# A two-layer mixture of experts on one core: the last group's down products two slots sooner, routing in single slots, first weights from ScalarE's queue, FFN tiles shared anew

## The chip, the cores and the metric

The kernel runs on one core of a Trainium2 chip. The time is the device time of one execution in microseconds (us). The engines are TensorE (PE in the profile, PEld for its weight loads), VectorE (DVE), ScalarE (ACT), GpSimd (POOL) and SyncE (SP, which here only issues transfers).

## The reference

There are 32 samples of 128 tokens with 128 channels, all in fp32. Two layers each add an FFN output to x:

```python
x = x + _L0_ffn_ref(_L0_cond_ref(x, cond_1024, ...), ...)
x = x + _L1_ffn_ref(_L1_cond_ref(x, cond_1024, ...), ...)
```

- Layer 0's first half gives each sample two of four experts by a gate: `out += w_be * mask[e] * (gelu(x @ ew1[e] + eb1[e]) @ ew2[e] + eb2[e])`, and adds a shared expert `gelu(x @ sw1 + sb1) @ sw2 + sb2`.
- Layer 0's second half runs eight experts on every token, `silu(x @ w_gate) * (x @ w_up) @ w_down`, weighted per token by the product of two softmaxes, normalized.
- Layer 1's first half has two shared silu experts and eight routed gelu experts, of which each token takes two by a sigmoid router.
- Layer 1's second half is a low-rank FFN: `gelu((x @ U1) @ V1 + b1) @ U2 @ V2 + b2`.

## The kernel before

The tokens stand as 8 blocks of 512 columns. Every matmul operand is split into a high and a low part (fp32r), and each product takes three matmuls: high by high, weight low by input high, weight high by input low. The work is a list of tiles, `plan()`, of 128 hidden channels by 512 columns. A tile goes up (its product lands in one of four PSUM banks, `zb`), through an activation, is split into `HH` and `HL` (two of the three other engines), and goes down (three matmuls, two in layer 1) into an output bank.

The kinds of tiles, in program order: A (the shared expert of layer 0, blocks 0 to 5), G (19 groups of four samples, gathered by expert, 4 tiles each), A again (blocks 6 and 7), B (8 experts by 8 blocks by 4 tiles), then S, R and F (layer 1: shared, routed, and the final low-rank FFN with tiles f = 0 to 3 per block).

Order is set by slots. Slot k holds, on TensorE, first the small products that stand in tables for k (`route_a` and others), then the up product of tile k, then the down product of tile k - LAG, with LAG = 5. The other engines walk the same slots in their own programs, each strictly in its own order. k0 below is the slot in which the last group's (G18's) first tile goes up; the A tiles of block 6 go up at k0+4 to k0+7, those of block 7 at k0+8 to k0+11, and B's first at k0+12.

What hangs on the last group: after its fourth down product at slot t_g (before: k0+8), VectorE forms `TMP` (L1266: bank plus bias, times the mask and weight `WM`), GpSimd adds it to four samples in `AC` (L1479, four adds), and only then may the routing matmuls of layer 0 read `AC` (L755, in `route_a`, from slot t_g+3 on) and ScalarE and VectorE split `AC` into the `XH` and `XL` of B (L911 and L1291, `split_a`). `WM` for the group is made by GpSimd (L1463) in the slot five after the group's second tile went up; this place is not changed. The routing of four blocks feeds a softmax (`soft_a`, `exp_a`, L919).

An `inplace` tile is activated within its PSUM bank, and its bank is free only when its `HL` is written. Any other tile's activation goes to `Hf`, which has NS = 4 places by tile number modulo 4, so that tile n waits for the `HL` of tile n - 4. `hi_act` says that ScalarE writes `HH` (L968), else VectorE does (L1395); `lo_pool` says that GpSimd writes `HL` (L1469), else VectorE does (L1398). In the F tiles of the last three blocks (`LATE` = 5), tiles 0 and 2 have `HH` from VectorE and `HL` from GpSimd; tile 1 is in place with `HH` from ScalarE and `HL` from VectorE; tile 3 is in place with both from VectorE. These twelve tiles are the end of the program.

At the start, SP issues x's first block, the first half of the first weights, the small constants and the second half of those weights, then the rest of x. TensorE runs two fp32 matmuls on zeros (`WARM`, L706), for which GpSimd clears part of `AC` (L1404). The first product needs x split by VectorE (L1278, L1280) and the weights split by ScalarE (L897) and VectorE (L1283).

Of the kernel before, what the change touches and what calls it, by code (L numbers as in the profile page):

```python
# [12 lines left out]
NB = 32  # L13
NT = NB * P
BLK = 512
NBLK = NT // BLK
SEG = (0, 42, 86, 128)
LATE = NBLK - 3
LAG = 5
# [17 lines left out]
AW = 1024  # L37
# [6 lines left out]
NGRP = 19  # L44
NPAIR = 4 * NGRP
FRONT = 6
# [8 lines left out]
class Item:  # L55


    def __init__(self, kind, blk, ex, f, last):
        self.kind, self.blk, self.ex, self.f, self.last = kind, blk, ex, f, last
        self.cols = BLK  # L60
        self.inplace = kind in "AG" or (kind == "F" and blk >= LATE and f % 2 == 1)

# [50 lines left out]
def build(nc, x_d, small_d, pack_d, wa_d, wb_d, wc_d, wf_d, scr_d, wup_d, wdown_d, out_d):  # L113
    with ExitStack() as ctx:
# [39 lines left out]
        AC = sb("AC", [P, NB + 4, P], F32, actx)  # L154
# [34 lines left out]
        f_wa = [sem(f"f_wa{i}") for i in range(5)]  # L189
# [7 lines left out]
        s_zero = sem("s_zero")  # L197
# [23 lines left out]
        items = plan()  # L221
# [4 lines left out]
        real = [it for it in items if it]  # L226
        for n, it in enumerate(real):
            it.n = n
        pos = {(it.kind, it.blk, it.ex, it.f): it for it in real}

        def done(kind, blk, ex, f):
            return pos[kind, blk, ex, f].k + LAG

        t_g = done("G", NGRP - 1, 0, 3)
# [5 lines left out]
        def when(times, after=0):  # L240
            return {t + after: b for b, t in enumerate(times)}

        split_a = {t_g + 3 + b: b for b in range(NBLK)}
        route_a = {t_g + 3: (0,), t_g + 4: (1,), t_g + 5: (2, 3), t_g + 8: (4,), t_g + 9: (5,), t_g + 10: (6,),
                   t_g + 12: (7,)}
        logit_a = {t + 1: v[-1] // 4 for t, v in route_a.items() if v[-1] % 4 == 3}
        lag_b = [t + (4 if b % 4 == 3 else 5) for b, t in enumerate(t_b)]
        split_b, route_b, logit_b = when(t_b, 2), when(lag_b), when(lag_b, 1)

        soft_a = {t_g + 6: 0, t_g + 14: 1}  # L250
        soft_at = {}
# [40 lines left out]
        read = {}  # L292
        for it in real:
            if it.last and it.kind in "AGB":
                late = 3 if (it.kind, it.blk, it.ex) == ("B", 0, 0) else 0
                read.setdefault(it.k + LAG + late, []).append(it)


        z_users = []
        for k in range(slots):  # L300
            if k < len(items) and items[k]:
                it = items[k]
# [7 lines left out]
        for it in real:  # L310
            if it.kind in "BS":
                n_prod[it.n] = len(n_prod) + 1
            if it.kind == "R":
                n_gated[it.n] = len(n_gated) + 1
            it.hi_act = it.kind in "BS" or (it.kind in "AG" and it.k % (8 if it.k < 16 else 4) != 0) or (
                it.kind == "F" and (it.f == 1 if it.blk >= LATE else it.k % 2 == 1)) or (it.kind == "R" and it.ex % 4 != 3)
            it.lo_pool = (it.kind == "B" and it.k % 4 == 1) or (
# [200 lines left out]
        stage_a = [ST[:, 0, 0:AW], ST[:, 1, 0:AW], CWB[:, 0, 0:AW], CWB[:, 0, AW:2 * AW], CWB[:, 1, 0:AW]]  # L518
# [48 lines left out]
        def sync_program(e):  # L567
            e.dma_start(XT[:, 0, :], x_d[:, 0:BLK]).then_inc(f_x[0], 16)
            e.dma_start(stage_a[0][:, 0:512], wa_d[:, 0:512]).then_inc(f_wa[0], 16)
            e.dma_start(sm[:, 0:SOON], small_d[:, 0:SOON]).then_inc(f_sm, 16)  # L570
            e.dma_start(stage_a[0][:, 512:AW], wa_d[:, 512:AW]).then_inc(f_wa[1], 16)
            for b in range(1, NBLK):
# [8 lines left out]
            for k in range(slots):  # L581
# [53 lines left out]
                if k in fill_b:  # L635
                    ex = fill_b[k]
# [28 lines left out]
                if k in add_y:  # L665
                    b = add_y[k]
                    e.wait_ge(*ab_done.of(("y", b)))
                    e.dma_start(out_d[:, b * BLK:b * BLK + BLK], CB[:, b % 2, :]).then_inc(f_out[b], 16)
                if LAG <= k < len(items) + LAG and items[k - LAG]:
                    it = items[k - LAG]  # L670
# [32 lines left out]
        def tensor_program(e):  # L703
# [4 lines left out]
            for k in range(slots):  # L708
# [53 lines left out]
                if k in route_b:  # L762
                    b = route_b[k]
# [24 lines left out]
                if k in last_mm:  # L788
                    b = last_mm[k]
# [4 lines left out]
                if k < len(items) and items[k]:  # L794
                    up(e, items[k])
                if LAG <= k < len(items) + LAG and items[k - LAG]:
                    down(e, items[k - LAG])

# [91 lines left out]

        def scalar_program(e):
            e.wait_ge(s_zero, 1)
            e.activation(q1[0:NB, :], AC[0:NB, 4 * FRONT, :], ACT.Gelu_apprx_tanh)
# [9 lines left out]
            for k in range(slots):  # L903
# [3 lines left out]
                if k in split_a:  # L907
                    b = split_a[k]
# [12 lines left out]
                if k in split_b:  # L921
                    b = split_b[k]
# [7 lines left out]
                if k in low_rank:  # L930
                    b = low_rank[k]
# [471 lines left out]
        def gpsimd_program(e):  # L1403
            e.memset(AC[:, 4 * FRONT:NB + 4, :], 0.0).then_inc(s_zero, 1)  # L1404
            e.wait_ge(s_wa_hi, 2)
# [174 lines left out]
```

## Time and profile before

| | us |
|---|---|
| median of 3 runs | 905.75 |
| lowest and highest | 904.97 and 907.12 |
| the profiled execution's own time | 907.58 |
| its span (first to last instruction) | 905.5 |
| TensorE busy | 882.8 |
| VectorE busy | 688.2 |
| ScalarE busy | 574.8 |
| GpSimd busy | 390.6 |
| mean granted TensorE clock | 0.994 |

Busy time counts the instructions of an engine and not its waits. The granted clock is the share of TensorE's 2.4 GHz that it was given; it has two levels, 1 (2.4 GHz) and 0.5 (1.2 GHz). In a timeline row the first number is the start from the beginning of the span, the second the duration, and the bracket at its end how long the engine had been idle and what ended that.

### The profile page before, as it was taken

How to read it: one execution, taken by the hardware profiler on the slowest of the kernel's cores; microseconds unless marked ns; L12 is line 12 of the kernel's file. 1: busy time of each engine (PE TensorE's matmuls, PEld its weight loads, DVE VectorE, ACT ScalarE, POOL GpSimd, SP SyncE). 2: the span in 40 equal slices, each digit the busy share in tenths (PEclk: the TensorE clock that was granted, in tenths of full speed). 3: DMA queues.
4: the chain of work that ended last, by engine and by line, in shares of the span. 5: the costliest groups of instructions: out<-in, count | busy, mean ns of one | idle time of the engine just before them, and what ended most of it. 6: DMA issues, size and time to landing. Idle time of an engine off the chain costs nothing.

```text
span 905.5 us, 12448 instructions
## 1 busy us (share of the span) xinstructions
PE 882.8 (97%) x3830; PEld 702.0 (78%) x3830; DVE 688.2 (76%) x1072; ACT 574.8 (63%) x997; POOL 390.6 (43%) x362
## 2 busy tenths in 40 slices
PE   8999999999999999999999999999999999999996
PEld 5778788787888888888888888888888776777773
DVE  7767777678778777677777676686676886998887
ACT  6777777675555455555555555555555677989896
POOL 7424644114445544244253243342322226754465
PEclk9999999899999999999999999999999999999999
DMA  9599994022012210111012012011010048171550
GB/s 304 186 276 313 315 305 142 1 84 99 33 47 100 91 47 40 42 47 54 28 47 75 8 47 82 1 47 47 0 47 1 1 87 194 32 182 47 164 104 36
DMA packets 36401, 86.15 MB, mean 95 GB/s; under 512 B 4464, under 2 KB 15472, under 8 KB 34416
## 3 DMA queue, kind: packets, MB, share of 16 engines
q1 hardware_dynamic: 36336, 85.37, 30.1%
q8 instruction: 30, 0.49, 0.2%
q14 instruction: 35, 0.29, 0.1%
HBM read 68.84 MB, written 6.83 MB: 84 GB/s over the span
## 4 chain that ended last, share of the span: by engine, by line
PE 80%; DVE 8%; ACT 4%; issue 4%; DMA 3%; POOL 1%; SPq 0%; DVEq 0%; ACTq 0%; POOLq 0%
PE ps L835 17%; PE ps L852 16%; PE ps L840 16%; PE ps L882 9%; PE ps L889 8%; PE ps L887 8%; DMA CWB<-scratch 2%; DVE HL L1398 2%; PE ps L869 1%; PE ps L867 1%; ACT HH L968 1%; DVE Hf L1386 1%; POOL HL L1469 1%; DVE HH L1395 1%; DVE Hf L1379 1%
## 5 line engine op out<-in xcount | busy, mean ns | idle before, releaser
L962 ACT ACTIVATE Sg<-ps 128x512 f32<-128x512 f32 x288 | 171.6, 597 | 246.1 <-PE ps L852 245.6
L1379 DVE TENSOR_TENSOR Hf<-ps,Sg 128x512 f32<-128x512 f32 x288 | 198.0, 688 | 150.8 <-ACT Sg L962 101.5
L1469 POOL TENSOR_TENSOR HL<-Hf,HH 128x512 fp32r<-128x512 f32 x136 | 182.1, 1345 | 172.2 <-ACT HH L968 155.4
L968 ACT ACTIVATE HH<-Hf 128x512 fp32r<-128x512 f32 x346 | 216.2, 625 | 23.1 <-DVE Hf L1379 14.6
L1398 DVE TENSOR_TENSOR HL<-Hf,HH 128x512 fp32r<-128x512 f32 x242 | 213.9, 884 | 4.2 <-ACT HH L968 3.2
L835 PE MATMUL ps<-XHL,WBH 128*128 128x512 f32 x512 | 203.8, 398 | 1.2 <-DVE Hf L1379 1.2
L852 PE MATMUL ps<-XHL,WBH 128*128 128x512 f32 x512 | 202.5, 396 | 0.0
L840 PE MATMUL ps<-XHL,WBL 128*128 128x512 f32 x512 | 202.1, 395 | 0.0
L1484 POOL TENSOR_TENSOR XT<-XT,TMP 128x512 f32<-128x512 f32 x64 | 83.5, 1304 | 250.3 <-DVE TMP L1275 250.3
L835 PEld LDWEIGHTS ps<-XHL,WBH 128*128 128x128 f32 x512 | 96.5, 188 | 24.0 <-DVE Hf L1379 2.3
L852 PEld LDWEIGHTS ps<-XHL,WBH 128*128 128x128 f32 x512 | 96.5, 188 | 22.5
L840 PEld LDWEIGHTS ps<-XHL,WBL 128*128 128x128 f32 x512 | 96.5, 188 | 22.1
L1398 DVE TENSOR_TENSOR HL<-ps,HH 128x512 fp32r<-128x512 f32 x114 | 78.4, 689 | 40.5 <-ACT HH L968 37.5
L882 PE MATMUL ps<-HH,WBH 128*128 128x512 f32 x256 | 101.2, 395 | 0.0
L889 PE MATMUL ps<-HL,WBH 128*128 128x512 f32 x256 | 100.8, 394 | 0.0
L887 PE MATMUL ps<-HH,WBL 128*128 128x512 f32 x256 | 100.3, 392 | 0.0
L955 ACT ACTIVATE ps<-ps,GWU 128x512 f32<-128x512 f32 x76 | 50.3, 662 | 27.5 <-PE ps L852 27.5
L1479 POOL TENSOR_TENSOR AC<-AC,TMP 128x128 f32 x76 | 32.7, 462 | 59.6 <-DVE TMP L1266 59.5
L882 PEld LDWEIGHTS ps<-HH,WBH 128*128 128x128 f32 x256 | 48.1, 188 | 11.5 <-DVE TMP L1275 0.3
L889 PEld LDWEIGHTS ps<-HL,WBH 128*128 128x128 f32 x256 | 48.0, 188 | 11.5
L887 PEld LDWEIGHTS ps<-HH,WBL 128*128 128x128 f32 x256 | 48.1, 188 | 11.2
L835 PE MATMUL ps<-XHL,WCH 128*128 128x512 f32 x128 | 51.7, 404 | 2.8 <-ACT Sg L962 1.5
(244 smaller groups left out, 1324.7 us busy)
## 6 DMA issues: line engine op xcount, KB each, us to landing
CWB<-scratch SPq DMA_DIRECT2D x68, 256.0 KB, 7.3
CWB<-scratch SPq DMA_DIRECT2D x15, 1024.0 KB, 4.7
GWD<-expert_down SPq DMA_DIRECT2D x19, 576.5 KB, 5.8
GWU<-expert_up SPq DMA_DIRECT2D x19, 514.0 KB, 5.5
GX<-XHL SPq DMA_DIRECT2D x76, 128.0 KB, 4.0
ST<-in_wb_dram SPq DMA_DIRECT2D x8, 768.0 KB, 6.3
XT<-in_x_dram SPq DMA_DIRECT2D x8, 256.0 KB, 5.4
expert_up<-GWU SPq DMA_DIRECT2D x4, 512.0 KB, 4.5
```

Of the source, the lines that this page charges most:

```text
L835: e.matmul(o, wh, tokens(it, 0), start=True, stop=False)
L840: e.matmul(o, wl, tokens(it, 0), start=False, stop=False)
L852: e.matmul(o, wh, tokens(it, 1), start=False, stop=True).then_inc(s_z, 1)
L882: e.matmul(bk[:, 0:n], wh, HH[:, hs, 0:n], start=it.new, stop=False)
L887: e.matmul(bk[:, 0:n], wl, HH[:, hs, 0:n], start=False, stop=False)
L889: e.matmul(bk[:, 0:n], wh, HL[:, hs, 0:n], start=False, stop=it.last).then_inc(s_down, 1)
L962: e.activation(Sg[:, it.n % NG, :], zb[z % NZ][:, :], ACT.Silu).then_inc(s_act, 1)
L968: e.activation(HH[:, it.n % NH, 0:it.cols], hidden_place(it), ACT.Copy).then_inc(s_hi_act, 1)
L1379: e.tensor_tensor(Hf[:, it.n % NS, :], zb[z % NZ][:, :], Sg[:, it.n % NG, :], ALU.mult).then_inc(s_prod, 1)
L1398: e.tensor_tensor(l, f, h.bitcast(F32), ALU.subtract).then_inc(s_lo_dve, 1)
L1469: e.tensor_tensor(HL[:, it.n % NH, :], Hf[:, it.n % NS, :], HH[:, it.n % NH, :].bitcast(F32), ALU.subtract).then_inc(s_lo_pool, 1)
L1484: e.tensor_tensor(XT[:, it.blk, :], XT[:, it.blk, :], TMP[:, t % 2, :], ALU.add).then_inc(s_acc, 1)
```

## The change

There are four edits.

1. The down products of the last group's tiles 1, 2 and 3 come 1, 1 and 2 slots sooner. With that t_g moves from k0+8 to k0+6, and all that is counted from it. The splits of blocks 0 to 5 come two slots sooner, those of blocks 6 and 7 stay. The routing of blocks 2 and 3, which shared a slot, gets two; that of blocks 4 to 7 stays in its slots k0+16 to k0+20. The first softmax comes one slot sooner, the second stays. B's first sum is read one slot sooner.
2. The two halves of the first weights are issued from ScalarE's queue, ahead of all else there.
3. GpSimd's clearing of `AC` is cut in two, and the warming matmuls wait for the first third only.
4. Of the last twelve F tiles, tile 3 of blocks 5 and 6 is no longer in place: its activation goes to `Hf`, `HH` comes from VectorE out of `Hf`, and `HL` from GpSimd. Tile 3 of block 7 stays in place, with `HH` from ScalarE.

```diff
@@ class Item
-        self.inplace = kind in "AG" or (kind == "F" and blk >= LATE and f % 2 == 1)
+        self.inplace = kind in "AG" or (kind == "F" and blk >= LATE and (f == 1 or f == 3 and blk == NBLK - 1))
@@ build
+        downs = {}
+        for it in real:
+            near = {1: 1, 2: 1, 3: 2}.get(it.f, 0) if it.kind == "G" and it.blk == NGRP - 1 else 0
+            it.d = it.k + LAG - near
+            downs.setdefault(it.d, []).append(it)
+
         def done(kind, blk, ex, f):
-            return pos[kind, blk, ex, f].k + LAG
+            return pos[kind, blk, ex, f].d
...
-        split_a = {t_g + 3 + b: b for b in range(NBLK)}
-        route_a = {t_g + 3: (0,), t_g + 4: (1,), t_g + 5: (2, 3), t_g + 8: (4,), t_g + 9: (5,), t_g + 10: (6,),
-                   t_g + 12: (7,)}
+        split_a = {t_g + 3 + b if b < FRONT else t_g + 5 + b: b for b in range(NBLK)}
+        route_a = {t_g + 3: (0,), t_g + 4: (1,), t_g + 5: (2,), t_g + 6: (3,), t_g + 10: (4,), t_g + 11: (5,),
+                   t_g + 12: (6,), t_g + 14: (7,)}
...
-        soft_a = {t_g + 6: 0, t_g + 14: 1}
+        soft_a = {t_g + 7: 0, t_g + 16: 1}
...
-                late = 3 if (it.kind, it.blk, it.ex) == ("B", 0, 0) else 0
-                read.setdefault(it.k + LAG + late, []).append(it)
+                late = 2 if (it.kind, it.blk, it.ex) == ("B", 0, 0) else 0
+                read.setdefault(it.d + late, []).append(it)
...
-                it.kind == "F" and (it.f == 1 if it.blk >= LATE else it.k % 2 == 1)) or (it.kind == "R" and it.ex % 4 != 3)
+                it.kind == "F" and (it.inplace if it.blk >= LATE else it.k % 2 == 1)) or (it.kind == "R" and it.ex % 4 != 3)
@@ sync_program
-            e.dma_start(stage_a[0][:, 0:512], wa_d[:, 0:512]).then_inc(f_wa[0], 16)
             e.dma_start(sm[:, 0:SOON], small_d[:, 0:SOON]).then_inc(f_sm, 16)
-            e.dma_start(stage_a[0][:, 512:AW], wa_d[:, 512:AW]).then_inc(f_wa[1], 16)
@@ tensor_program
-                if LAG <= k < len(items) + LAG and items[k - LAG]:
-                    down(e, items[k - LAG])
+                for it in downs.get(k, ()):
+                    down(e, it)
@@ scalar_program
+            e.dma_start(stage_a[0][:, 0:512], wa_d[:, 0:512]).then_inc(f_wa[0], 16)
+            e.dma_start(stage_a[0][:, 512:AW], wa_d[:, 512:AW]).then_inc(f_wa[1], 16)
@@ gpsimd_program
-            e.memset(AC[:, 4 * FRONT:NB + 4, :], 0.0).then_inc(s_zero, 1)
+            e.memset(AC[:, 4 * FRONT:4 * FRONT + 4, :], 0.0).then_inc(s_zero, 1)
+            e.memset(AC[:, 4 * FRONT + 4:NB + 4, :], 0.0).then_inc(s_zero, 1)
```

Line numbers of the changed kernel are 5 to 8 higher from L755 on: L835, L840 and L852 (up products) are L840, L845 and L857 there, L882, L887 and L889 (down products) are L887, L892 and L894, and L755 (routing) is L760.

On TensorE, between the last group's last down product and the first routing, the program before has these rows (`GWD` is the group's down weight, `WAS` that of A); the first is the last down matmul of the group, in slot k0+8:

```order
L889 MATMUL ps<-HL,GWD 128x512
L835 MATMUL ps<-XHL,WAS 128x512
L840 MATMUL ps<-XHL,WAS 128x512
L852 MATMUL ps<-XHL,WAS 128x512
L882 MATMUL ps<-HH,WAS 128x512
L887 MATMUL ps<-HH,WAS 128x512
L889 MATMUL ps<-HL,WAS 128x512
L835 MATMUL ps<-XHL,WAS 128x512
L840 MATMUL ps<-XHL,WAS 128x512
L852 MATMUL ps<-XHL,WAS 128x512
L882 MATMUL ps<-HH,WAS 128x512
L887 MATMUL ps<-HH,WAS 128x512
```

The third down matmul of that slot and the first routing, `L755 MATMUL ps<-sm,AC 128x16 x4`, come next, so that 12 large matmuls stand between. The changed kernel has this at the same place, from the last group's last two down products on:

```order
L894 MATMUL ps<-HL,GWD 128x512
L887 MATMUL ps<-HH,GWD 128x512
L892 MATMUL ps<-HH,GWD 128x512
L894 MATMUL ps<-HL,GWD 128x512
L840 MATMUL ps<-XHL,WAS 128x512
L845 MATMUL ps<-XHL,WAS 128x512
L857 MATMUL ps<-XHL,WAS 128x512
L840 MATMUL ps<-XHL,WAS 128x512
L845 MATMUL ps<-XHL,WAS 128x512
L857 MATMUL ps<-XHL,WAS 128x512
L760 MATMUL ps<-sm,AC 128x16 x4
```

Two up products, 6 large matmuls, are left between the last group's end and the first routing; two down products and two up products that stood ahead of it now follow it, the downs of the group having been drawn together.

On VectorE, at the end of the program, before (`ps1` and `ps3` are the banks of tiles 1 and 3, `PS` the low-rank input of block 7, `QS` that of an output):

```order
L1395 CAST HH<-Hf 128x512
L1395 CAST HH<-ps3 128x512
L1398 TENSOR_TENSOR HL<-ps3,HH 128x512
L1356 SCALAR_TENSOR_TENSOR PS<-PH,sm,ps4 128x512
L1395 CAST HH<-Hf 128x512
L1398 TENSOR_TENSOR HL<-ps1,HH 128x512
L1395 CAST HH<-Hf 128x512
L1395 CAST HH<-ps3 128x512
L1398 TENSOR_TENSOR HL<-ps3,HH 128x512
L1364 SCALAR_TENSOR_TENSOR QS<-PH,sm,ps7 128x512
```

and in the changed kernel:

```order
L1402 CAST HH<-Hf 128x512 x2
L1363 SCALAR_TENSOR_TENSOR PS<-PH,sm,ps4 128x512
L1402 CAST HH<-Hf 128x512
L1405 TENSOR_TENSOR HL<-ps1,HH 128x512
L1402 CAST HH<-Hf 128x512 x2
L1371 SCALAR_TENSOR_TENSOR QS<-PH,sm,ps7 128x512
```

The `HL` of tile 3 of blocks 5 and 6 has left VectorE for GpSimd, whose run of `HL` at the end grows from 72 to 74, and the cast of tile 3 reads `Hf` in place of the bank.

## Rows read from the trace of the kernel before

**Rows 1.** The page, part 1: busy us, share of the span, instructions.

```profile
PE 882.8 (97%) x3830; PEld 702.0 (78%) x3830; DVE 688.2 (76%) x1072; ACT 574.8 (63%) x997; POOL 390.6 (43%) x362
```

**Rows 2.** Busy time by stretch: us, engines, granted clock (PEclk), DMA share, GB/s.

```profile
165.00:175.00 10.00, 10.00 (x43) 8.58 (x43) 3.83 (x6) 5.00 (x8) 0.00 (x0) 0.66 0.01 2
300.00:700.00 400.00, 400.00 (x1752) 325.08 (x1751) 287.87 (x412) 213.29 (x383) 152.25 (x118) 1.00 0.11 40
880.00:905.50 25.50, 17.09 (x60) 10.02 (x58) 20.53 (x32) 15.75 (x27) 14.09 (x11) 0.93 0.18 53
```

**Rows 3.** Instructions in order of time, 0 to 10 us: start, us, engine, line.

```profile
0.74 1.38 POOL L1404 MEMSET AC<- 128x1536 f32 x1 [0.29 <-POOLq L1564]
...
4.07 0.43 DVE L1278 CAST XHL<-XT 128x512 fp32r<-128x512 f32 x1 [4.07 <-DMA XT<-in_x_dram]
...
4.69 0.63 ACT L897 ACTIVATE WAS<-ST 128x512 fp32r<-128x512 f32 x1 [2.23 <-DMA ST<-in_wa_dram]
5.36 0.69 DVE L1283 TENSOR_TENSOR WAS<-ST,WAS 128x512 fp32r<-128x512 f32 x1
...
6.18 0.72 PE L840 MATMUL ps<-XHL,WAS 128*128 128x512 f32 x1
```

**Rows 4.** The same, 157 to 163 us, around the last group's sum.

```profile
157.67 1.04 POOL L1463 TENSOR_TENSOR WM<-GWD,WP 128x512 f32<-128x512 f32 x1
...
157.92 0.39 PE L835 MATMUL ps<-XHL,WAS 128*128 128x512 f32 x1
...
159.06 0.39 PE L889 MATMUL ps<-HL,GWD 128*128 128x512 f32 x1
...
160.62 0.74 DVE L1266 SCALAR_TENSOR_TENSOR TMP<-ps,GWD,WM 128x512 f32<-128x512 f32 x1
...
161.54 1.70 POOL L1479 TENSOR_TENSOR AC<-AC,TMP 128x128 f32 x4 [2.83 <-DVE TMP L1266]
```

**Rows 5.** The same for TensorE alone, 163 to 166 us.

```profile
163.39 1.04 PE L755 MATMUL ps<-sm,AC 128*128 128x16 f32 x8 [1.16 <-POOL AC L1479]
...
165.18 0.63 PE L882 MATMUL ps<-HH,WAS 128*128 128x512 f32 x1
```

**Rows 6.** The same for TensorE, around 306 us.

```profile
306.41 2.76 PE L785 MATMUL ps<-ST 128*128 128x32 f32 x24
```

**Rows 7.** The same, ScalarE at 167 us.

```profile
167.13 1.28 ACT L962 ACT_TABLE_LOAD   x1
```

**Rows 8.** The same, all engines, 886 to 902 us.

```profile
886.33 1.28 POOL L1469 TENSOR_TENSOR HL<-Hf,HH 128x512 fp32r<-128x512 f32 x1 [0.37 <-DVE HH L1395]
...
886.62 1.26 DVE L1395 CAST HH<-Hf 128x512 fp32r<-128x512 f32 x1 [0.38 <-ACT Hf L955]
...
887.97 1.27 POOL L1469 TENSOR_TENSOR HL<-Hf,HH 128x512 fp32r<-128x512 f32 x1 [0.36 <-DVE HH L1395]
...
889.33 0.69 ACT L955 ACTIVATE Hf<-ps,sm 128x512 f32<-128x512 f32 x1 [0.55 <-POOL HL L1469]
...
889.60 1.30 POOL L1469 TENSOR_TENSOR HL<-Hf,HH 128x512 fp32r<-128x512 f32 x1 [0.36 <-DVE HH L1395]
...
890.15 0.69 DVE L1398 TENSOR_TENSOR HL<-ps,HH 128x512 fp32r<-128x512 f32 x1
...
890.76 0.74 DVE L1356 SCALAR_TENSOR_TENSOR PS<-PH,sm,ps 128x512 fp32r<-128x512 f32 x1
...
891.41 0.42 DVE L1395 CAST HH<-Hf 128x512 fp32r<-128x512 f32 x1
...
891.91 1.28 POOL L1469 TENSOR_TENSOR HL<-Hf,HH 128x512 fp32r<-128x512 f32 x1 [1.01 <-DVE HH L1395]
...
897.52 1.29 POOL L1469 TENSOR_TENSOR HL<-Hf,HH 128x512 fp32r<-128x512 f32 x1 [0.36 <-DVE HH L1395]
...
898.86 0.50 PE L869 MATMUL ps<-HL,U2S 128*128 128x512 f32 x1 [0.45 <-POOL HL L1469]
...
901.38 0.47 PE L793 MATMUL ps<-QS,V2S 128*128 128x512 f32 x1 [1.33 <-DVE QS L1364]
```

## The prediction, made before the changed kernel was run

> **What bounds the kernel now.** I read the page's engine rows first: TensorE is busy for 97% of the span [rows 1]. The windows by stage come next. From 300 to 700 us TensorE never idles and issues 1752 matmuls in 400 us, 0.228 us each [rows 2]; I call this 0.23. So what TensorE waits, or does at a lower clock, is paid in full, and nothing else is. The windows show two such places: 165 to 175 us, where the granted clock was 0.66, and 880 to 905.5 us, where TensorE worked 17.09 of 25.50 us [rows 2]. The timeline adds a third, the start, where the first product waits for x and weights [rows 3]. The four edits touch just these three places, and the rest keeps its order. Each place has its own chain: GpSimd's sum of the last group before the routing [rows 4, 5]; the splits of the last F tiles at the end [rows 8]; at the start, VectorE behind the first transfer [rows 3].
>
> **Edit 1, the last group.** Before, the group's third down matmul of its last tile starts at 159.06. With it and the 12 large matmuls behind it, 13 x 0.23 = 2.99, TensorE is free at 162.05; the routing starts at 163.39 [rows 4, 5], so the wait is 1.34 (the profile's idle, by modelled ends, is 1.16). In the changed order two up products (6 matmuls, 1.38) move from ahead of the last down to behind it. So the last down comes 1.38 sooner, at 157.68, one slot's work and not two. Behind it stand 6 large matmuls, and TensorE is free at 157.68 + 7 x 0.23 = 159.29.
>
> When is the routing released? `TMP` (L1266) needs this down product, and also `WM`, whose instruction keeps its slot and ends at 157.67 + 1.04 = 158.71 [rows 4]. It stood out of the way of a `TMP` at 160.62; now it is what `TMP` waits for, so `TMP` starts at about 158.75. From `TMP` to the first routing took 163.39 - 160.62 = 2.77: `TMP` itself, the four adds that start at 161.54 and take 1.70, and hand-overs [rows 4, 5]. The routing is then released at 161.52. The wait is 161.52 - 159.29 = 2.23, against 1.34: **+0.9 us**. The routing comes 1.87 us sooner in time, but with 12 matmuls (2.76) less behind it. Bounds: if `TMP` waited for its down product alone (158.1), +0.25; if VectorE's queue holds it 0.7 us more (an `HL` ahead of it, whose input goes up 0.7 later now), +1.6.
>
> Queued behind the wait are ScalarE's split of block 0, then its activations, and VectorE's `HL` of the next tiles. In the changed order three splits more stand on ScalarE before the first B tile, and the silu table load of 1.28 [rows 7]. I walk ScalarE from 161.4 with a split at 0.63, as the copy in [rows 3], and about 0.66 for an activation: the `HL` of the last A tile is late by some 0.8 us for the bank of B's second tile. That holds at the full clock; at half of it TensorE comes later and the 0.8 is covered. Bounds 0 and 1.0.
>
> **The clock.** After 1.16 us of idle and eight small routing matmuls of 1.04 together, the next rows show 0.63 for a large matmul where 0.39 stood [rows 4, 5]: the clock fell to 1.2 GHz. By the window at 0.66 this took 10 x (1 - 0.66) = 3.4 us of full-speed work [rows 2]. Against that, 24 small matmuls in 2.76 us with no wait ahead of them, at 306 us, left the clock at 1.00 [rows 2, 6]. So the wait together with the routing decides, and the changed order has the longer wait, then a routing in each of the next three slots. I take it that the clock falls again, and for as long. One routing more than before then runs in the slow stretch; at half speed its 1.04 could double, and by half of that I add **+0.5** (bounds 0 and +2).
>
> **Edit 4, the tail.** The `HL` on GpSimd takes 1.28; they are at 887.97, 889.60, 891.91, ... 897.52, and TensorE's 898.86 waits for the last of them [rows 8]. Six such instructions stand between 887.97 and 898.81; the change makes them eight, 10.2 us of work in 10.8. A second thing counts: a cast out of `Hf` on VectorE that meets a GpSimd instruction stands until that ends. At 886.62 it took 1.26, to 887.88, which is 0.27 after GpSimd's end at 887.61; at 891.41, with GpSimd idle, it took 0.42 [rows 8]. The next `HL` starts 0.09 behind the cast.
>
> The walk, from rows that don't change (887.97, 889.60). Block 5, tile 2: GpSimd meets the new cast of tile 3, which I price at 0.25, half of the cast: end 891.13. Tile 3: 892.41. Block 6, tile 0: its cast can start at 891.17, since `PS` starts at 890.52 without the removed `HL` of 890.15 (0.24 gained), but it meets the new instruction and ends at 892.68; `HL` 892.77 to 894.05. Before it ended at 891.91 + 1.28 = 893.19: 0.86 late. Tile 2's cast stands behind that and ends at 894.32; `HL` to 895.94 with 0.25 for the next cast; tile 3 to 897.22. Block 7, tile 0: cast to 897.49, `HL` to 898.86; tile 2: cast to 899.13, `HL` 899.22 to 900.50. Before: 897.52 + 1.29 = 898.81. **+1.7 us**, and the last matmul at 901.38 and the output behind it move with it [rows 8]. What VectorE saves is 0.69 (the `HL`) a block, of which the walk uses 0.24. Bounds: +0.8 if the casts never meet GpSimd after the first block, +2.3 if both contend each time.
>
> I round this to +1.6, since the third block's tile 3 now has its cast on ScalarE and frees VectorE a little.
>
> **Edits 2 and 3, the start.** Before, x is there at 4.07 and VectorE splits it; ScalarE's weight copy starts at 4.69 and ends at 5.32; VectorE's low part of the weights starts at 5.36; TensorE's second matmul follows at 6.18 [rows 3]. If the weights land 0.5 sooner, VectorE is busy with x until 5.22, so the second matmul gains 0.14. Everything behind starts from it. The warming can start when a third of 1.38 is cleared, 0.9 sooner. The first rows are at the low clock (0.72 for a large matmul at 6.18), and an earlier warming may raise it sooner, up to 0.5. Against that, the weights now compete with x. Both were there by 4.69, so x lands between 4.07 and 4.69: up to +0.6. I take **0**, between -0.6 and +0.6.
>
> The Trainium skill, "DMA: Bandwidth & Descriptors", section "Queues, rings and completion order", says that SP and ACT each own a ring on the same 16 engines and that each engine goes round-robin between them; its section "Issuing engines are not separate DMA queues" adds that several issuing engines save sequencer time only. By that rule x and the weights would share from the first packet, and the start would be at the +0.6 end. The trace before has one issuing queue and can't show it.
>
> **The sum.** 0.9 + 0.5 + 1.6 + 0 = +3.0 us on the profiled execution's own 907.58, that is 910.6. That execution is 1.83 above the median of the runs, so for the median I take 905.75 + 3.0 = **908.8**.
>
> **The rivals.**
> - *The clock doesn't fall.* The stall stays, but the low stretch goes: -3.4 + 0.9 + 0.8 + 1.6 = -0.1, 905.7. For it: the three timed runs lie 2.1 us apart, so perhaps not each has the low stretch, and only one place in the trace has it. Against: the wait is longer. 0.18.
> - *The routing is released in time* (the faster side). If the sum of the group is there when TensorE is free, at 159.3 and not 161.5, the wait of 1.34 goes and the clock's fall with it: -1.3 - 3.4 + 1.6 = -3.1, 902.6. It decides if `TMP` to routing takes under about 0.6 us where 2.77 stood. Against it speak the four adds alone, 1.70 [rows 4]. 0.12, most of it for what I have not seen.
> - *GpSimd's two more instructions are hidden* in its idle time: +1.4, 907.2. For it: it idles 1.01 before 891.91. Against: that is filled by one instruction of 1.28. 0.08.
> - *x lands late.* The two queues share from the start: 908.8 + 0.6 = 909.4. 0.07 apart from the forecast.
> - *The clock stays low through all four routings*, +2 in place of +0.5, and the tail at its upper bound: 911. 0.05.
> - The forecast: 0.50, its own range 907.4 to 910.4.
>
> **The numbers.** A measurement of this kernel tells about 0.2%, 1.8 us, from no change. Slower takes the forecast but for 0.03, and the last two rivals: 0.47 + 0.12 = 0.59, with 0.01 of the third 0.60. Same is most of the first (0.15), the rest of the third and 0.03: 0.25. Faster is the second and 0.03 of the first: 0.15. The range from 904.6 to 911.2 leaves out the faster case and the far end of the last.
>
> **What would show it.** In the changed profile: the wait before the first routing about 2.2 us and `TMP` right behind `WM`; a stretch with the clock at 0.5 after it; eight `HL` on GpSimd at the end, almost without idle, and casts out of `Hf` of more than 1 us; the last GpSimd instruction some 1.7 us later against the last R tile. I am wrong if `TMP` to the routing is much shorter, if the clock stays up, or if GpSimd's instructions and VectorE's casts don't meet.

## The result, and the profile after

Both kernels ran 20 times on one chip. The changed kernel took 910.0 us (906.9 to 914.1), the kernel before 906.6 (903.9 to 910.3): a ratio of 1.0040, 95% interval 1.0027 to 1.0054. The means are 910.2 and 906.55. The forecast was 908.8, slower by 3.0 us; it is slower by 3.4 (medians) or 3.6 (means).

The profiled execution of the changed kernel is one of its quickest, with 908.26 of its own and a span of 906.1, only 0.7 and 0.6 above that of before. So its rows show the waits well, and the whole difference badly. The page and the windows of the changed kernel, columns as in [rows 1, 2]:

```profile
PE 882.4 (97%) x3830; PEld 701.3 (77%) x3830; DVE 688.1 (76%) x1069; ACT 575.3 (63%) x998; POOL 393.3 (43%) x365
```

```profile
160.00:170.00 10.00, 8.23 (x41) 7.24 (x42) 5.35 (x8) 4.97 (x10) 1.63 (x4) 0.83 0.01 2
165.00:175.00 10.00, 9.36 (x51) 7.76 (x51) 4.85 (x8) 7.69 (x14) 0.00 (x0) 0.96 0.01 2
300.00:700.00 400.00, 400.00 (x1754) 325.08 (x1752) 288.09 (x413) 213.53 (x382) 152.14 (x118) 1.00 0.11 39
880.00:906.10 26.10, 18.07 (x58) 10.87 (x57) 20.22 (x28) 16.21 (x28) 16.37 (x13) 0.88 0.16 50
```

GpSimd is 2.7 us busier, the two `HL` of 1.28. The bulk from 300 to 700 us is as it was. From 880 us to the end TensorE is busy 18.07 us in place of 17.09, at a granted clock of 0.88 in place of 0.93.

The last group, by the timeline (start, us, engine, line; the bracket is the idle time and what ended it), answering to [rows 4, 5]:

```profile
157.82 1.05 POOL L1471 TENSOR_TENSOR WM<-GWD,WP 128x512 f32<-128x512 f32 x1
157.85 0.39 PE L894 MATMUL ps<-HL,GWD 128*128 128x512 f32 x1
...
158.11 0.69 DVE L1405 TENSOR_TENSOR HL<-ps,HH 128x512 fp32r<-128x512 f32 x1 [0.81 <-ACT HH L975]
...
159.01 0.75 DVE L1273 SCALAR_TENSOR_TENSOR TMP<-ps,GWD,WM 128x512 f32<-128x512 f32 x1 [0.20 <-POOL WM L1471]
...
159.25 0.40 PE L857 MATMUL ps<-XHL,WAS 128*128 128x512 f32 x1
...
159.94 1.69 POOL L1487 TENSOR_TENSOR AC<-AC,TMP 128x128 f32 x4 [1.06 <-DVE TMP L1273]
...
161.77 1.32 PE L760 MATMUL ps<-sm,AC 128*128 128x16 f32 x8 [2.12 <-POOL AC L1487]
...
163.51 0.63 PE L845 MATMUL ps<-XHL,WAS 128*128 128x512 f32 x1
...
174.76 0.50 PE L840 MATMUL ps<-XHL,WBH 128*128 128x512 f32 x1 [0.64 <-DVE HL L1405]
```

`TMP` starts right behind `WM`. The last down product started 1.16 us ahead of it; the profile puts the end of VectorE's wait down to `WM`, not to it. TensorE is free at 159.25 + 0.23 = 159.48 and starts the routing at 161.77, a wait of 2.29 where 1.34 stood. Its next large matmuls run at 0.63, at 1.2 GHz. At 174.76 it waits for the late `HL`: 173.72 to 174.76 is 1.04 between two matmuls that stand 0.23 apart without a wait, 0.81 lost.

The start, answering to [rows 3]:

```profile
0.74 0.40 ACTq L897 DMA_DIRECT2D ST<-in_wa_dram  x1
0.74 0.52 POOL L1411 MEMSET AC<- 128x512 f32 x1 [0.29 <-POOLq L1572]
...
5.16 0.43 DVE L1285 CAST XHL<-XT 128x512 fp32r<-128x512 f32 x1 [5.16 <-DMA XT<-in_x_dram]
...
6.97 0.50 PE L845 MATMUL ps<-XHL,WAS 128*128 128x512 f32 x1 [0.46 <-DVE WAS L1290]
```

x lands 1.09 us later than at 4.07, the second matmul comes 0.79 later than at 6.18, and its 0.50 is a large matmul at the full clock, where 0.72 stood.

GpSimd alone in the tail, answering to [rows 8]:

```profile
887.54 1.27 POOL L1477 TENSOR_TENSOR HL<-Hf,HH 128x512 fp32r<-128x512 f32 x1 [0.36 <-DVE HH L1402]
889.17 2.65 POOL L1477 TENSOR_TENSOR HL<-Hf,HH 128x512 fp32r<-128x512 f32 x2 [0.36 <-DVE HH L1402]
892.19 1.29 POOL L1477 TENSOR_TENSOR HL<-Hf,HH 128x512 fp32r<-128x512 f32 x1 [0.36 <-DVE HH L1402]
893.84 2.65 POOL L1477 TENSOR_TENSOR HL<-Hf,HH 128x512 fp32r<-128x512 f32 x2 [0.36 <-DVE HH L1402]
896.86 1.28 POOL L1477 TENSOR_TENSOR HL<-Hf,HH 128x512 fp32r<-128x512 f32 x1 [0.36 <-DVE HH L1402]
898.51 1.28 POOL L1477 TENSOR_TENSOR HL<-Hf,HH 128x512 fp32r<-128x512 f32 x1 [0.36 <-DVE HH L1402]
```

Eight `HL`, from 887.54 to 899.79, 12.25 us; before the six took from 887.97 to 898.81, 10.84. That is +1.41. TensorE's last matmul is at 902.37, and was at 901.38 [rows 8].

Read along the program, the changed kernel's TensorE is level with before at the first wait for loaded weights (51.04 and 51.01). Around the routing it has the wait of +0.95 and the late `HL` of +0.81, and gets them back because its clock was low for a shorter stretch here (0.96 against 0.66 in the window from 165). It is level again at 209.6, and there it gains 0.47, at a wait that I had not looked at. Of the changed kernel and of the kernel before, TensorE's row behind that wait:

```profile
210.42 0.50 PE L840 MATMUL ps<-XHL,WBH 128*128 128x512 f32 x1 [0.44 <-DVE Hf L1386]
```

```profile
210.94 0.50 PE L835 MATMUL ps<-XHL,WBH 128*128 128x512 f32 x1 [0.92 <-DVE Hf L1379]
```

What moved is on VectorE's rows, of the kernel before and of the changed one:

```profile
203.43 0.68 DVE L1275 TENSOR_TENSOR TMP<-ps,CWB 128x512 f32<-128x512 f32 x1
```

```profile
198.82 0.68 DVE L1282 TENSOR_TENSOR TMP<-ps,CWB 128x512 f32<-128x512 f32 x1
```

Before, B's first sum stands directly ahead of the second softmax on VectorE, with the `Hf` that TensorE waits for behind both. In the changed kernel it is read one slot sooner and falls into idle time of VectorE, and all behind it comes sooner.

From there to the tail TensorE is 0.4 to 0.5 ahead, and the tail turns this into 1.0 behind.

### The profile page after: what moved, and what is told of

Its sections match the earlier page's. It is cut to its first block, busy times and chain, and to the rows that moved or that the text cites. A ratio compares the mean times of both kernels' runs of the same rounds, so it can differ in the third digit from the quotient of the medians.

```text
span 906.1 us, 12451 instructions
## 1 busy us (share of the span) xinstructions
PE 882.4 (97%) x3830; PEld 701.3 (77%) x3830; DVE 688.1 (76%) x1069; ACT 575.3 (63%) x998; POOL 393.3 (43%) x365
## 4 chain that ended last, share of the span: by engine, by line
PE 81%; DVE 8%; issue 4%; ACT 3%; DMA 2%; POOL 2%; POOLq 0%; DVEq 0%; ACTq 0%
PE ps L840 17%; PE ps L857 17%; PE ps L845 17%; PE ps L887 9%; PE ps L894 9%; PE ps L892 8%; DMA CWB<-scratch 2%; DVE HL L1405 2%; PE ps L874 1%; POOL HL L1477 1%; PE ps L872 1%; DVE Hf L1393 1%; DVE HH L1402 1%; DVE Hf L1386 1%; PE ps L760 1%
## 5 line engine op out<-in xcount | busy, mean ns | idle before, releaser
L1477 POOL TENSOR_TENSOR HL<-Hf,HH 128x512 fp32r<-128x512 f32 x138 | 184.8, 1345 | 173.1 <-ACT HH L975 157.8
L840 PE MATMUL ps<-XHL,WBH 128*128 128x512 f32 x512 | 203.3, 397 | 1.4 <-DVE Hf L1386 0.7
L857 PE MATMUL ps<-XHL,WBH 128*128 128x512 f32 x512 | 202.1, 395 | 0.0
L845 PE MATMUL ps<-XHL,WBL 128*128 128x512 f32 x512 | 201.6, 394 | 0.0
L840 PEld LDWEIGHTS ps<-XHL,WBH 128*128 128x128 f32 x512 | 96.2, 188 | 24.4 <-DVE Hf L1386 1.8
L857 PEld LDWEIGHTS ps<-XHL,WBH 128*128 128x128 f32 x512 | 96.2, 188 | 22.5
L845 PEld LDWEIGHTS ps<-XHL,WBL 128*128 128x128 f32 x512 | 96.2, 188 | 22.1
L887 PE MATMUL ps<-HH,WBH 128*128 128x512 f32 x256 | 101.1, 395 | 0.0
L894 PE MATMUL ps<-HL,WBH 128*128 128x512 f32 x256 | 100.8, 394 | 0.0
L892 PE MATMUL ps<-HH,WBL 128*128 128x512 f32 x256 | 100.3, 392 | 0.0
L894 PEld LDWEIGHTS ps<-HL,WBH 128*128 128x128 f32 x256 | 48.0, 188 | 11.6
L892 PEld LDWEIGHTS ps<-HH,WBL 128*128 128x128 f32 x256 | 48.1, 188 | 11.3
L887 PEld LDWEIGHTS ps<-HH,WBH 128*128 128x128 f32 x256 | 48.1, 188 | 11.2
L840 PE MATMUL ps<-XHL,WCH 128*128 128x512 f32 x128 | 51.7, 404 | 2.8 <-ACT Sg L969 1.5
```

The costliest lines, as they stand in the source:

```text
L840: e.matmul(o, wh, tokens(it, 0), start=True, stop=False)
L845: e.matmul(o, wl, tokens(it, 0), start=False, stop=False)
L857: e.matmul(o, wh, tokens(it, 1), start=False, stop=True).then_inc(s_z, 1)
L887: e.matmul(bk[:, 0:n], wh, HH[:, hs, 0:n], start=it.new, stop=False)
L892: e.matmul(bk[:, 0:n], wl, HH[:, hs, 0:n], start=False, stop=False)
L894: e.matmul(bk[:, 0:n], wh, HL[:, hs, 0:n], start=False, stop=it.last).then_inc(s_down, 1)
```

## The experiments

**How the clock enters.** Over the 20 runs of the changed kernel the mean granted clock goes from 0.985 to 0.997, and the time falls with it, with a correlation of -0.85. From each run's clock c and span s the time spent at 1.2 GHz is 2 (1 - c) s; a line through the runs of before gives 0.31 to 0.35 us of time for each us at the low clock (three sets, 96 runs). Below, "low" is the mean of that time, and "at an equal clock" is the mean time less 0.3 times the low. That is a fit and not a measurement of one stretch: the changed kernel's own 20 runs give 0.27 and the 12 of edit 1 alone 0.46, so a few tenths of a difference "at an equal clock" hang on the 0.3. It also counts low time wherever it falls, the tail included. The kernel before had low 6.7, 5.3 and 8.0 us in its three sets, each on its own chip, and 903.7, 903.0 and 903.9 us at an equal clock. The changed kernel had low 13.2 and 906.25 at an equal clock; its neighbour, the 20 runs of before, has no clocks on record.

### Each edit alone

The first four kernels, on one chip, are the kernel before with one edit of the diff above: edit 1 whole; edit 4's two lines; edit 2's lines moved; edit 3's memset cut.

> Edit 1 alone on the kernel before. Theory A (the prediction's sum): the wait before the first routing is 2.2 to 2.3 us in place of 1.3, the clock falls behind it in most executions, and the time is 0.9 to 1.9 us above before (+0.1 to +0.2%). Rival B (the clock stays up, or its low stretch is shorter, as in the profile of the changed kernel with 3.4 us in place of 6.8): -1.7 to +0.3 us. Rival C (most of the measured +3.4 us comes from here, through a low stretch in nearly every execution): +2.5 us or more.

> Edit 4 alone on the kernel before. Theory A (GpSimd's two more HL instructions and the casts that meet them): from the HL of block 5's tile 0 to the end of the last HL on GpSimd 12.2 us in place of 10.8, and the time +1.4 to +1.7 us. Rival B (the tail is hidden and the difference comes from elsewhere): within 0.5 us of before. Rival C (TensorE's clock also falls in the tail, as the changed kernel's profile shows from 889.4 us on, and this adds): over +2 us.

> Edit 2 alone on the kernel before. Theory A (the weights in ScalarE's queue share the transfer engines with x): x's first block is there at about 5.2 us in place of 4.1, VectorE's first HH some 0.4 to 1.0 us later, and the time +0.2 to +1.0 us. Rival B (later waits for transfers, like the one at 51 us, take the delay up): within 0.2 us of before.

> Edit 3 alone on the kernel before. Theory A: the warming matmuls start at 1.3 in place of 2.2 us, the clock is up before the first product in more executions, and VectorE's first HH comes up to 0.5 us sooner; the time -0.5 to 0 us. Rival B (the start is bound by the x transfer and by VectorE alone): no difference.

| kernel | median | ratio to before (95%) | low | at equal clock, against before (903.7) |
|---|---|---|---|---|
| edit 1 alone | 909.16 | 1.0027 (1.0007 to 1.0047) | 11.7 | +1.8 |
| edit 4 alone | 906.86 | 1.0016 (0.9998 to 1.0033) | 9.7 | +0.8 |
| edit 2 alone | 905.19 | 0.9988 (0.9972 to 1.0003) | 7.2 | -0.8 |
| edit 3 alone | 905.46 | 1.0008 (0.9987 to 1.0028) | 7.8 | +0.3 |

The ratios are not those of the medians. The last column's errors are 0.35 to 0.6 us each, from the scatter of the runs alone; with its own slope of 0.46, edit 1 would have +1.0 there. Only edit 1's interval leaves out 1; the other three can't be told from no change by their times, and are read by their rows. Edit 1 costs 2.4 us by the ratio and 3.3 by the medians, more than the 0.9 to 1.9 of its theory A and nearer to rival C, with low 11.7 in place of 6.7. The four add up to +2.1, the whole change has +2.6 at an equal clock. The rest of its +3.6 is, by this fit, time at the low clock; a second way to that share comes below.

TensorE with edit 1 alone, from the last product before the routing:

```profile
160.24 0.40 PE L859 MATMUL ps<-XHL,WAS 128*128 128x512 f32 x1
162.75 1.50 PE L762 MATMUL ps<-sm,AC 128*128 128x16 f32 x8 [2.12 <-POOL AC L1486]
164.10 0.77 PE L842 MATMUL ps<-XHL,WAS 128*128 128x512 f32 x1
...
175.34 1.72 PE L762 MATMUL ps<-sm,AC 128*128 128x16 f32 x8
...
177.90 0.63 PE L859 MATMUL ps<-XHL,WBH 128*128 128x512 f32 x1
```

The wait is the same 2.28, but in this execution the clock stays low through all four routings, the rival that I gave 0.05: large matmuls take 0.63 up to the one that starts at 179.60. In the changed kernel's own profile it was back after one. The same wait, then, is followed by low stretches of very different length, and the mean over runs is what counts.

With edit 4 alone the eight `HL` on GpSimd go from 889.24 to 901.46, 12.22 us, as its theory A had it. With edit 2 alone x lands at 4.54 (0.47 later, and not at the 5.2 expected), and the time is not longer: its theory A falls. With edit 3 alone the warming starts at 1.32 in place of 2.17, but VectorE's first `HH` comes at 4.06 and came at 4.07. Large matmuls take 0.39 there from 6.42 on, where before it was 7.95; but they do so from 6.53 on with edit 4 alone too, whose start is that of before. So nothing can be put down to edit 3.

What follows from the start is drowned by something else. Between 50 and 107 us TensorE waits once to three times ahead of matmuls on a group's weights, and these waits differ between executions. The profile puts some down to the transfer of the weights and most, as this one, to nothing that it shows, so that they are waits for loading is my reading. Here one stands where before has none:

```profile
57.59 0.39 PE L887 MATMUL ps<-HL,GWD 128*128 128x512 f32 x1
59.01 0.48 PE L833 MATMUL ps<-GX,GWU 128*128 128x512 f32 x1 [1.03 <-issue]
```

To weigh the start with all that runs into it, I take from each profiled execution of this study when GpSimd makes `WM` of group 16, a point ahead of all that edits 1 and 4 touch. Of the kernel before, of one with its start as before (the tail run with six `HL`), and of one with edit 2 (with the downs moved too, told below):

```profile
146.52 1.05 POOL L1463 TENSOR_TENSOR WM<-GWD,WP 128x512 f32<-128x512 f32 x1
```

```profile
148.73 1.05 POOL L1463 TENSOR_TENSOR WM<-GWD,WP 128x512 f32<-128x512 f32 x1
```

```profile
145.77 1.05 POOL L1468 TENSOR_TENSOR WM<-GWD,WP 128x512 f32<-128x512 f32 x1
```

The nine executions without edit 2 have 146.5 to 148.7, mean 147.6. The four with it have 145.8, 146.7, 147.3 and 148.3, mean 147.0. The spread of 2.2 to 2.5 us is larger than any effect of edits 2 and 3, and the late x can't be seen in it.

### Is it the wait that lowers the clock?

Idle TensorE time can be filled without moving any other engine. Into the wait ahead of the first routing I put large matmuls whose results are overwritten, nine in the changed kernel, five in the kernel before:

```diff
+                        if b == 0:
+                            for _ in range(9):
+                                e.matmul(bk[:, :].rearrange("p (s t) -> p s t", t=P), expert_weights(0, 0)[0][:, 0:P],
+                                         XS[:, NB - 4:NB, 0, :], start=True, stop=True)
```

> The changed kernel with nine large matmuls into the routing bank (overwritten by the routing; the output is the same) in the wait of 2.2 us before the first routing. The wait and the order stay, only TensorE is kept at work. Theory A (the longer wait makes the clock fall more often and for longer, and this is about 2 us of the 3.4 to 4.5 us that the changed kernel loses): the mean time at the low clock falls from 13 us to 7 or less, and the time is 1.5 to 2.5 us below the changed kernel's 910.0. Rival B (the low clock comes from the four routings, each small, in four slots in a row, not from the wait): time within 0.7 us of the changed kernel.

> The kernel before with five such matmuls in its wait of 1.3 us. Theory A: its clock falls less often, the mean time at the low clock goes from 7 us to 4 or less, and the time is 0.6 to 1.5 us below before. Rival B: no difference.

The changed kernel with fillers took 906.1 us, 1.0019 of before on that chip (1.0005 to 1.0033), with low 3.9 in place of 13.2. The kernel before with fillers took 904.1, a ratio of 1.0001 (0.9988 to 1.0014), low 5.0 (5.3). TensorE of the changed kernel with fillers:

```profile
160.05 2.26 PE L759 MATMUL ps<-XHL,WAS 128*128 128x512 f32 x9
162.26 1.06 PE L764 MATMUL ps<-sm,AC 128*128 128x16 f32 x8
163.18 0.48 PE L844 MATMUL ps<-XHL,WAS 128*128 128x512 f32 x1
...
163.73 0.39 PE L861 MATMUL ps<-XHL,WAS 128*128 128x512 f32 x1
```

The routing comes no sooner (3.84 us behind the last down product, 3.92 without fillers), and the matmuls behind it run at 0.39. The other profiled executions agree. From 162 to 182 us the granted clock was 0.57 to 0.91 in all three that have a wait of 2.0 to 2.3 us, 0.83 in three of the six that have the wait of 1.3 and 1.00 in the other three, and 1.00 in all four in which TensorE doesn't idle there (the two with fillers and the two of the next section). So the longer wait does lower the clock more often.

For the price, take the pair with fillers, on one chip: 906.2 and 904.4 in the mean, 1.8 us apart (give or take 0.8). Without fillers the two kernels are 3.65 apart. So the clock costs the changed kernel about 1.9 us of its 3.6, with an error of some 1.4, as the pairs are from two chips. In the kernel before, the fillers gain nothing that can be measured, in time or in low: its theory A, 0.6 to 1.5 us, falls. What low time it has on this chip must then lie mostly elsewhere; where, the mean doesn't tell.

### Can edit 1 be had without its wait?

The downs of the last group moved as in edit 1, but the routing, the splits and the softmax left in their old slots:

```diff
+        downs = {}
+        for it in real:
+            near = {1: 1, 2: 1, 3: 2}.get(it.f, 0) if it.kind == "G" and it.blk == NGRP - 1 else 0
+            it.d = it.k + LAG - near
+            downs.setdefault(it.d, []).append(it)
...
-                read.setdefault(it.k + LAG + late, []).append(it)
+                read.setdefault(it.d + late, []).append(it)
...
-                if LAG <= k < len(items) + LAG and items[k - LAG]:
-                    down(e, items[k - LAG])
+                for it in downs.get(k, ()):
+                    down(e, it)
```

> The down products of the last group moved as in edit 1, and its sum read with them, but the routings, splits and softmaxes left in the slots of the kernel before. Theory A (the loss of edit 1 is that the routing follows the sum by as many slots as before, over slots with half the work): the sum is there at about 161.5 and TensorE is free at 162.1, so the wait of 1.3 us goes; -1.0 to -1.5 us from the wait, more if the clock stays up: -1.3 to -2.5 us against before. Rival B (drawing the down products together costs as much elsewhere, through the banks and HL of the A tiles): within 0.7 us of before or slower.

It took 903.5 us, a ratio of 0.9991 (0.9976 to 1.0006), with -1.4 at an equal clock (give or take 0.6). By the rows the wait is gone; the time alone can't be told from no change. The wait at 210 us stands at 0.95 here, as before: this kernel reads B's first sum in its old place. Then the same with edit 2's lines as well:

> The kernel before with two things: the downs of the last group 1, 1 and 2 slots sooner with all routing, splits and softmax left in their old slots (as in the run of the moved downs alone), and the first weights issued from ScalarE's queue (as in the run of that alone). Theory A: both gains stand and are in different places, so they add: the wait before the first routing gone (TensorE's gap there about 1.0, the routing itself), load waits of the start absorbed; time about 1.5 to 2.5 below before at an equal clock, 902 to 903 where before is at 904.5, ratio 0.998. Rival B: what either alone showed (0.999 each) was chance, and the ratio is 1.000 within 0.001.

It took 901.8 us (901.3 to 903.3, 9 runs; before 906.3), a ratio of **0.9952** (0.9934 to 0.9969), with low 3.4 and -3.1 at an equal clock. This beats both kernels, by more than theory A's 0.998. Of the 4.5 us to before, 1.4 are low time by the fit: before had low 8.0 in this set. TensorE at the place, from the group's last down product:

```profile
156.94 0.39 PE L892 MATMUL ps<-HL,GWD 128*128 128x512 f32 x1
...
161.30 0.39 PE L892 MATMUL ps<-HL,WAS 128*128 128x512 f32 x1
161.53 0.96 PE L758 MATMUL ps<-sm,AC 128*128 128x16 f32 x8
162.34 0.48 PE L838 MATMUL ps<-XHL,WAS 128*128 128x512 f32 x1
```

No wait, and no low clock. The group's sum is there in time, since 18 large matmuls now stand between the group's last down and the routing, where before had 12 and the changed kernel 6. So it is not the sooner downs that cost, but the routing that was drawn forward with them. The two parts alone, -1.4 and -0.8, come to less than the -3.1 together; each has an error of 0.3 to 0.4, so the 0.9 between is not clear of noise, and I don't know of a reason why they should help each other.

### Who holds TMP?

In the kernel with edit 1 alone, `WM` of the last group is made ahead of the four adds of the group before it, and not behind them:

```diff
-                if ... items[k - LAG].kind == "G" and items[k - LAG].f == 1:
-                    g = items[k - LAG].blk
+                if ... items[k - LAG].kind == "G" and (
+                        items[k - LAG].f == 1 or (items[k - LAG].blk, items[k - LAG].f) == (NGRP - 2, 3)):
+                    g = items[k - LAG].blk + (items[k - LAG].f == 3)
...
```

> The kernel with edit 1 alone, and GpSimd makes WM of the last group ahead of the four adds of the group before it and not behind them. Theory A: WM holds TMP by no more than the 0.20 us that its row shows, since an HL on VectorE stands ahead of TMP and ends only then; TMP starts 0.2 to 0.25 sooner and the wait before the first routing goes from 2.3 to about 2.05. Rival B, as the prediction had it: TMP would be free to start with its down product, 0.65 sooner, and the wait is 1.6 or less; the clock then may stay up. Time within 1 us of the run with edit 1 alone in both, but for the clock.

It took 907.7 us, 1.0014 of before (0.9990 to 1.0037). VectorE, and TensorE on both sides of the wait:

```profile
158.75 0.69 DVE L1405 TENSOR_TENSOR HL<-ps,HH 128x512 fp32r<-128x512 f32 x1 [0.81 <-ACT HH L975]
159.36 0.74 DVE L1273 SCALAR_TENSOR_TENSOR TMP<-ps,GWD,WM 128x512 f32<-128x512 f32 x1
```

```profile
159.90 0.40 PE L859 MATMUL ps<-XHL,WAS 128*128 128x512 f32 x1
162.12 1.04 PE L762 MATMUL ps<-sm,AC 128*128 128x16 f32 x8 [1.82 <-POOL AC L1489]
```

The wait is 162.12 - 160.13 = 1.99 and was 2.28: 0.29 shorter, as theory A had it. `TMP` now stands directly behind an `HL` on VectorE. So with `WM` out of the way a second holder is left, which gives only 0.29 us, and the prediction's lower bound of +0.25 on the wait was out of reach: 1.99 is 0.65 above the 1.34 of before.

### What is it in the tail?

The prediction had two causes mixed: GpSimd has two instructions more, and the casts that read `Hf` wait for GpSimd. Two kernels part them. The first is edit 4 with the `HL` of tile 3 left on VectorE:

```diff
-                it.kind == "F" and (not it.inplace if it.blk >= LATE else it.k % 2 == 1)) or (
+                it.kind == "F" and (it.f % 2 == 0 if it.blk >= LATE else it.k % 2 == 1)) or (
```

> The kernel before with edit 4, except that the HL of tile 3 of blocks 5 and 6 stays on VectorE (read from Hf) and GpSimd keeps its six HL at the end. Theory A: what costs 1.4 us in edit 4 are GpSimd's two more instructions of 1.28; with VectorE doing them, GpSimd's run from the HL at about 888 to the end of its last returns to 10.8 to 11.3 us (12.2 with the whole of edit 4), time within 0.5 us of before at an equal clock. Rival B: it is the way over Hf (casts and subtractions on VectorE that take 1.25 when they meet GpSimd, 0.4 to 0.7 otherwise), and the run stays at 12 us or more, +1 us or more.

It took 907.6 us, 1.0012 of before (0.9995 to 1.0028), +1.2 at an equal clock. GpSimd has six `HL` again, from 886.97 to 899.22, and they take 12.25 us, no less than the eight. This is rival B. VectorE shows why:

```profile
888.89 1.65 DVE L1398 TENSOR_TENSOR HL<-Hf,HH 128x512 fp32r<-128x512 f32 x1
890.46 0.74 DVE L1356 SCALAR_TENSOR_TENSOR PS<-PH,sm,ps 128x512 fp32r<-128x512 f32 x1
891.12 0.42 DVE L1395 CAST HH<-Hf 128x512 fp32r<-128x512 f32 x1
```

The subtraction from `Hf` takes 1.65 and ends 0.55 behind GpSimd's `HL` of 888.60 to 889.99; from a bank it takes 0.69. GpSimd then idles 1.62 for the cast behind it, and does so once more a block later. So theory A falls: the two more instructions on GpSimd are not what costs by itself. With all of edit 4 GpSimd has 10.4 us of work and idles 1.8; here it has 7.9 and idles 4.3, in the same stretch. Whoever does it, a tile 3 that goes over `Hf` puts work into a chain in which VectorE and GpSimd take turns.

The second keeps tile 3 in place in all three blocks, and gives its `HH` to ScalarE:

```diff
-                it.kind == "F" and (it.f == 1 if it.blk >= LATE else it.k % 2 == 1)) or (it.kind == "R" and it.ex % 4 != 3)
+                it.kind == "F" and (it.f % 2 == 1 if it.blk >= LATE else it.k % 2 == 1)) or (it.kind == "R" and it.ex % 4 != 3)
```

> The kernel before with HH of tile 3 of the last three blocks from ScalarE in place of VectorE; HL stays on VectorE and GpSimd keeps its six HL. Theory A (the tail is bound by the chain VectorE, GpSimd, ScalarE around Hf, and VectorE's 0.68 us a block are on it): the stretch from block 5's first HL to the last one's end on GpSimd shrinks from 10.8 by up to 1.3 us, and the time is 0.3 to 1.3 us below before. Rival B (ScalarE's copy delays the activation of the next tile, which the chain also needs): within 0.3 us.

It took 905.1 us, 1.0013 of before (0.9996 to 1.0029). The six `HL` take from 885.69 to 897.29, 11.6 us, 0.76 more than before, so theory A falls, and it is more than rival B's "no change". VectorE shows where it goes:

```profile
888.26 0.69 DVE L1398 TENSOR_TENSOR HL<-ps,HH 128x512 fp32r<-128x512 f32 x1 [1.02 <-ACT HH L968]
```

VectorE waits 1.02 us for ScalarE's `HH`, which itself stands behind an activation, and the next cast out of `Hf` is queued on VectorE behind this `HL`. From the block's first `HL` on GpSimd that cast starts 3.83 us later, and before it was 3.44: 0.39 lost a block, in two blocks.

## Why the prediction was right

- **The wait before the routing** was forecast at 2.23 and measured at 2.29 and 2.28, by the mechanism named: `WM` keeps its slot and `TMP` stands behind it. Right.
- **The late `HL`** for B's second tile, 0.8 at the full clock and covered at the low one: 0.81 in the changed kernel, and no such wait in the profile of edit 1 alone, where the clock was low. It stays with the fillers (0.81). Right, but the step put it into no term, as I took the clock to be low there; in the profiled run it was paid.
- **A gain that was missed**: the wait of 0.92 at 210 us is 0.44 in the changed kernel and 0.43 with edit 1 alone, 0.92 with edit 2 alone and 0.95 with the moved downs alone. It belongs to the part of edit 1 that reads B's first sum a slot sooner, by the rows of VectorE; no run changes this line alone.
- **The clock, "+0.5"**: this is the term that was mis-sized. I compared one low stretch with another, as if each execution had the same. It is a matter of how often and for how long: low 5.3 to 8.0 us on average in the sets of before and 13.2 after. The pairs with and without fillers put it at about +1.9, close to the upper bound given, and show that the wait is behind it. That the two profiled executions go the other way (0.66 before and 0.96 after in the window from 165) says how little one trace tells of this.
- **The tail, "+1.6"**: the walk gave +1.69 and the rows show +1.41 (1.38 with the edit alone). In the time of edit 4 alone +0.8 is left, at the edge of what can be told. The size was near. Of the two reasons, GpSimd's eight instructions ("10.2 us of work in 10.8") are not needed for it, as six take as long; the turns of VectorE and GpSimd at `Hf` are.
- **The start, "0"**: x landed at 5.16, outside the bounds of 4.07 and 4.69, which I had taken from when both transfers were there before. The weights were no sooner for it. By the Trainium skill, "DMA: Bandwidth & Descriptors", section "Queues, rings and completion order", the two rings share the 16 engines by turns, and the traces agree in direction for x: ready at 4.54 and 4.64 in the two profiled executions with edit 2 and not edit 3, at 5.16 and 5.02 in the two with both, at 3.95 to 4.20 in the nine without edit 2. Why edit 3 should add to it is open; alone it has 4.06. Yet edit 2 alone is not slower (0.9988), and four executions with it reach group 16 no later than nine without. What takes up the 0.5 to 1.1 was not found; the varying waits at 50 to 107 us may. The slow large matmuls of the first 8 us (0.63) don't show in the granted clock, which is 1.00 from 0 to 10 us before, so "low" doesn't hold them.
- **The rivals**: "the clock doesn't fall" stood 0.1 below before; with the fillers the changed kernel stands 1.9 above it in the medians. The rival took the 3.4 us of one profile's low stretch as a cost of every execution of before, and filling that kernel's wait gains 0.1. "Released in time" needs the routing in its old slot. Without edit 4, which this kernel leaves out, its sum is 4.7 below before. The kernel that does it was 0.7 below before, and 4.5 with edit 2 as well, on a chip where before had more low time.

The mechanisms of the wait and of the tail's turns were right, but that the sum came out near 3.4 is in part luck. A clock term too small by some 1.4 and a late `HL` of 0.8 that stood in no term were set against a tail 0.2 to 0.8 too large, the 0.5 at 210 us, and a start that may have given 0.5 (edits 2 and 3 alone: -0.8 and +0.3, neither told from nothing). As a check, without the clock's share the rows give 0.95 + 0.81 + 1.41 - 0.47 = +2.7, or +2.2 with that 0.5, and the pair with fillers is 1.8 apart, give or take 0.8.

## What to carry to other kernels

When a producer is moved forward, move its consumer only as far as the producer's result moves: `TMP` came 1.6 us sooner, the routing lost 2.8 us of work ahead of it. Ask what stood second in line behind the wait that you take away, on each engine. And where an idle stretch on TensorE can tip the clock, count the low time over many runs: a filler of useless matmuls, or real work left ahead of the wait, is the test.

## What the runs showed of the hardware

- The same stretch of program with the same wait (2.3 us without a matmul, then small ones) had a low stretch that ended at 165.6 in the changed kernel's execution and at 180.0 in that of edit 1 alone. The mean low time went from 6.7 to 11.7 us, on one chip, when edit 1 made the wait 2.28 in place of 1.34.
- A VectorE cast that reads `Hf` in SBUF while GpSimd works on SBUF stands until GpSimd's instruction ends: up to 1.34 where it takes 0.42 alone. A subtraction of two SBUF tensors takes 1.65 to 1.67 there and 0.68 alone (at 202.83 before). With the first operand in a PSUM bank both take 0.68 to 0.69 under the same GpSimd work.
- Issued from two queues at once, the first block of x was ready at 4.54 and 4.64 (edit 2 without edit 3) and at 5.16 and 5.02 (with it), and at 4.07 before. The weights were not earlier for it: ScalarE's copy of them began at 4.72 and 4.82, and at 5.33 and 5.21, and at 4.69 before.
